# Adapter weights formed per sample and multiplied in two tiles of the array, in a four-layer conditioned network

## What is computed

```python
dg, db = c @ down_gamma, c @ down_beta        # [64, 64] each
ug, ub = c @ up_gamma,   c @ up_beta          # [64, 256] each
w_down = down_project[None] * dg[:, None, :] + db[:, None, :]     # [B, 256, 64]
w_up   = up_project[None]   * ug[:, None, :] + ub[:, None, :]     # [B, 64, 256]
up = einsum('bsh,bhd->bsd', relu(einsum('bsd,bdh->bsh', x, w_down)), w_up)
x = x + up
x = x + L1(x)     # x plus a product with weights of rank 30, decoded per sample
x = x + L2(x)     # a modulated projection, attention (16 heads, in each token), another projection
x = x + L3(x)     # table norms, three small networks, a gated two-layer network, a norm
```

## Time and profile before

| | |
|---|---|
| median of 3 runs | 538.26 us (537.77 to 538.40) |
| span of the profiled execution | 537.6 us |
| what the three runs have around that span | 0.2 to 0.8 us |
| PE busy | 462.3 us, 86% |
| DVE, ACT, POOL busy | 65%, 53%, 32% |
| moved by DMA | 61.0 MB, mean 113 GB/s |

### The profile page before, as it was taken

The page is one execution under the profiler, slowest core; times in us unless marked ns, Lnnn a source line. Parts: engine busy times, 40 slices in busy tenths (PEclk is TensorE's granted clock), DMA queues, the critical chain, the costliest instruction groups (busy, mean ns, idle before and its releaser), DMA issues.

```text
span 537.6 us, 9360 instructions
## 1 busy us (share of the span) xinstructions
PE 462.3 (86%) x3768; PEld 259.2 (48%) x3768; DVE 347.5 (65%) x653; ACT 282.6 (53%) x421; POOL 170.1 (32%) x146
## 2 busy tenths in 40 slices
PE   3896668924899999999999999999999898849981
PEld 3673335512365546554555654565546555424431
DVE  0374547593387488749856983898388778454923
ACT  0201488262853976578756966793976497102100
POOL 3009895110304232413231323314231420172121
PEclk9998767986599999999999999999999999879986
DMA  5991700331733713553183338143713561320011
GB/s 152 341 265 57 193 1 21 92 97 52 186 97 84 231 57 106 160 154 88 76 215 99 119 81 212 69 157 69 207 41 122 139 166 54 101 78 19 0 40 39
DMA packets 68736, 61.00 MB, mean 113 GB/s; under 512 B 53910, under 2 KB 55572, under 8 KB 68308
## 3 DMA queue, kind: packets, MB, share of 16 engines
q1 hardware_dynamic: 64404, 43.86, 30.0%
q0 software_dynamic: 3712, 12.59, 7.4%
q10 hardware_dynamic: 576, 3.95, 2.0%
HBM read 39.18 MB, written 21.07 MB: 112 GB/s over the span
## 4 chain that ended last, share of the span: by engine, by line
PE 67%; DVE 14%; issue 5%; DMA 5%; SPq 4%; ACT 3%; POOL 2%; POOLq 0%; DVEq 0%; ACTq 0%
PE ph L750 17%; PE pk L729 10%; PE pp L712 5%; PE ph L712 4%; PE ph L838 3%; PE pp L759 3%; PE pp L871 2%; PE pp L854 2%; DVE kx L1621 2%; PE pp L810 2%; PE pk L720 2%; PE pk L648 1%; PE ph L648 1%; PE pk L750 1%; DMA bd<-in_w_dec 1%
## 5 line engine op out<-in xcount | busy, mean ns | idle before, releaser
L1140 ACT ACTIVATE bd<-vc,ownrow 128x512 f32<-128x512 f32 x124 | 78.3, 711 | 0.0
L1127 ACT ACTIVATE bd<-kc,ownrow 128x512 f32<-128x512 f32 x120 | 75.6, 709 | 0.3
L447 POOL TENSOR_TENSOR demod<-demod,neghalf 128x32 f32<-128x32 f32 x8 | 43.4, 5448 | 35.2 <-DVE demod L1382 35.2
L729 PEld LDWEIGHTS pk<-bd,kc 128*32 128x32 f32 x1024 | 30.4, 120 | 17.1 <-issue 11.7
L729 PE MATMUL pk<-bd,kc 128*32 128x128 f32 x1024 | 35.4, 298 | 3.2 <-ACT bd L1127 3.2
L485 POOL TENSOR_TENSOR attnT<-attnT,style 128x1024 f32<-128x1024 f32 x6 | 11.4, 1901 | 76.4 <-DMA attnT<-av_dram 76.4
L712 PE MATMUL pp<-ys,kwT 128*128 128x512 f32 x64 | 30.6, 623 | 2.6 <-DVE ys L1604 2.6
L729 PE MATMUL pk<-bd,et 128*32 128x128 f32 x1024 | 31.1, 273 | 0.0
L729 PEld LDWEIGHTS pk<-bd,et 128*32 128x32 f32 x1024 | 27.2, 110 | 3.6 <-issue 3.2
L750 PE MATMUL ph<-tT,w 128*128 128x512 f32 x56 | 27.3, 633 | 0.1
L750 PE MATMUL ph<-x2T,w 128*128 128x512 f32 x56 | 25.9, 605 | 1.2 <-DVE h L1698 1.2
(11 more groups left out here) (348 smaller groups left out, 976.3 us busy)
## 6 DMA issues: line engine op xcount, KB each, us to landing
xin<-in_x SPq DMA_DIRECT2D x8, 512.0 KB, 4.5
x_dram<-x SPq DMA_DIRECT2D x8, 512.0 KB, 2.6
k_dram<-kxb SPq DMA_DIRECT2D x16, 256.0 KB, 3.3
kt<-k_dram SPq DMA_DIRECT2D x8, 512.0 KB, 4.0
v_dram<-kxb SPq DMA_DIRECT2D x8, 512.0 KB, 5.0
vt<-v_dram SPq DMA_DIRECT2D x8, 512.0 KB, 5.8
x1r<-x_dram SPq DMA_DIRECT2D x8, 512.0 KB, 3.5
av_dram<-av SPq DMA_DIRECT2D x8, 512.0 KB, 5.8
```

Of the source, the lines that this page charges most:

```text
L447: gp.tensor_tensor(q, q, neghalf[:, 0:4 * CB].rearrange("p (l a b) -> p l a b", l=2, a=2), ALU.pow).then_inc(gs_dem, 1)
L729: ins = mm(pk[32 * r:32 * r + 32, o:o + 128], weights(h, 4 * i + r)[:, 16 * pair:16 * pair + 32], bd[:, h, 8 * i + 2 * r + pair, :], start ...
L1127: fn(bd[:, h, :, 16 * b:16 * b + 16].rearrange("p (q z) x -> p q z x", z=2), kc[:, 16 * h:16 * h + 16, :].rearrange("p q (z x) -> p q z x" ...
L1140: fn(bd[:, h, :, 16 * b:16 * b + 16], vc[:, SH * h:SH * h + SH, :], ACT.Copy, scale=ownrow[:, 1, b:b + 1]).then_inc(s, 1)
```

## The change

- The factors of all samples are computed with samples on partitions, copied to `cond_rows`, stored to two DRAM tensors, and read back for each chunk broadcast over partitions: `down_gb` [128, 2, 512] by one transfer (512 KB) and `up_gb` [128, 2, 1024] by two transfers of 64 partitions (512 KB each). SP issues them at the end of step a for chunk a+1, the second pair after a wait on `p_up`.
- For each chunk GpSimd forms `w_down` (multiply, add; [128, 1024] each) and `w_up` (multiply, add; [128, 1024] each). Chunk 0's `w_down` is formed on DVE. Chunks 1 and 2 are formed between and behind the demodulation; chunk a+1 in steps a = 2 to 6: down behind the scaling of attnT, up behind the output store.
- The down product is 16 matmuls of 64 columns, alternating between two column tiles of 64; the up product 16 matmuls of 64 columns, alternating between two row tiles of 64. Relu is one ACT operation of 128x256 straight from PSUM. DVE adds 2x and the product in two operations (`stt`).
- The beta products, `row_in`, `row_mid` and their four DVE operations are gone, as are the columns of ones.
- `ys` shares `xT`'s buffer, `x1` shares `x0`'s, `kxb` shares `kx`'s; the waits move with them (`v_kx` now waits for both stores of the chunk before).
- In step 0 `first_factor(0)` and `(1)` come ahead of the down product.

```diff
+            sp.wait_ge(vs_par, 1)
+            sp.dma_start(down_dram.rearrange("g b h -> b g h"), cond_rows[:, 0:2 * H0].rearrange("b (g h) -> b g h", g=2)
+                         ).then_inc(d_rows, 16)
+            sp.dma_start(up_dram.rearrange("g b d -> b g d"), cond_rows[:, 2 * H0:].rearrange("b (g d) -> b g d", g=2)
+                         ).then_inc(d_rows, 16)
+            sp.wait_ge(d_rows, 32)
+            down_rows(0)
+            up_rows(0)
             for dst, src in late_loads:
...
                     sp.dma_start(xin[:, :, :], t["x"][:, (a + 1) * NT:(a + 2) * NT, :]).then_inc(d_x, 16)
+                    down_rows(a + 1)
+                    up_rows(a + 1)
...
+            def sample_down(c):
+                after(gp, d_dgb, c, 16)
+                after(gp, p_down, c - 1)
+                settled(gp)
+                gp.tensor_tensor(w_down[:, :, :].rearrange("p k (b h) -> p k b h", h=H0),
+                                 down_proj[:, :, :].unsqueeze(2).to_broadcast([128, 2, CB, H0]), by_sample(down_gb[:, 0, :]),
+                                 ALU.mult).then_inc(w_da, 1)
+                after(gp, w_da, c)
+                gp.tensor_tensor(w_down[:, :, :].rearrange("p k (b h) -> p k b h", h=H0),
+                                 w_down[:, :, :].rearrange("p k (b h) -> p k b h", h=H0), by_sample(down_gb[:, 1, :]),
+                                 ALU.add).then_inc(w_d, 1)
...
+            def sample_up(c):
+                after(gp, d_ugb, c, 32)
+                settled(gp)
+                gp.tensor_tensor(w_up.rearrange("p (b d) -> p b d", d=D), w_up.rearrange("p (b d) -> p b d", d=D),
+                                 up_proj[:, :].unsqueeze(1).to_broadcast([128, CB // 2, D]), ALU.mult).then_inc(w_ua, 1)
+                after(gp, w_ua, c)
+                gp.tensor_tensor(w_up, w_up, up_gb[:, 1, :], ALU.add).then_inc(w_u, 1)
...
+            gp.wait_ge(s_load, LAYERS)
+            sample_up(0)
             gp.wait_ge(vs_ss, 1)
-            demodulation(0, 4)
+            demodulation(0, 1)
+            sample_down(1)
+            sample_up(1)
+            demodulation(1, 4)
             networks()
             demodulation(4, NC)
             def step(n, a, v, d, e):
+                if a is not None and a == 1:
+                    sample_down(2)
+                    sample_up(2)
...
                                      ALU.mult).then_inc(g_ao, 1)
+                if a is not None and 1 < a < NC - 1:
+                    sample_down(a + 1)
...
                     gp.dma_start(out[:, e * NT:e * NT + NT, :], yn[:, :, :]).then_inc(d_out, 16)
+                if a is not None and 1 < a < NC - 1:
+                    sample_up(a + 1)
...
                     after(pe, a_xT, a)
+                    after(pe, w_d, a)
                     after(pe, v_hT, a - 3)
-                    for k in range(2):
-                        ins = mm(P0, w_down[:, k, :], xT[:, k, :], start=(k == 0), stop=(k == 1))
+                    for i in range(4):
+                        for k in range(2):
+                            for r in range(2):
+                                q = 4 * r + i
+                                ins = mm(P0[64 * r:64 * r + 64, S * i:S * i + S], w_down[:, k, H0 * q:H0 * q + H0],
+                                         xT[:, k, S * q:S * q + S], start=(i == 0 and k == 0), stop=(i == 3 and k == 1),
+                                         skip_group_check=True)
...
                     after(pe, a_act0, a)
+                    after(pe, w_u, a)
                     after(pe, a_hnT, a - 3)
-                    for o in range(2):
-                        mm(P23[:, 512 * o:512 * o + 512], w_up[:, 128 * o:128 * o + 128], act0, start=True, stop=True)
-                    mm(P0[64:128, :], w_up[:, D:D + H0], act0, start=True, stop=True).then_inc(p_up, 1)
+                    for i in range(4):
+                        for o in range(2):
+                            for r in range(2):
+                                z = slice(64 * r, 64 * r + 64)
+                                q = 512 * r + 256 * o + S * i
+                                ins = mm(P23[:, q:q + S], w_up[z, D * i + 128 * o:D * i + 128 * o + 128],
+                                         act0[z, S * i:S * i + S], start=(i == 0 and o == 0), stop=(i == 3 and o == 1),
+                                         skip_group_check=True)
...
-                if a is not None:
-                    after(pe, v_row_mid, a)
-                    for o in range(2):
-                        ins = mm(P01[:, 512 * o:512 * o + 512], ub_rows[64:128, 128 * o:128 * o + 128], row_mid, start=True, stop=True)
-                    ins.then_inc(p_ub, 1)
...
+                if a is not None:
+                    after(act, p_down, a)
+                    fn(act0[:, :], P0[:, 0:N // 2], ACT.Relu).then_inc(a_act0, 1)
                 if e is not None:
                     after(act, p_hid, e)
...
                     after(ve_, p_up, a)
-                    tt(by_batch(row_mid), by_batch(P0[64:128, :]), per_batch(batch_eye[64:128, :], B, a), ALU.mult
-                       ).then_inc(v_row_mid, 1)
-                    tt(by_batch2(x0[:, :, :]), by_batch2(halves(P23)), per_batch2(ug[:, :, :], a), ALU.mult
-                       ).then_inc(v_up, 1)
+                    after(ve_, d_x1w, a - 1, 16)
+                    for r in range(2):
+                        z = slice(256 * r, 256 * r + 256)
+                        stt(x0[:, :, z], xT[:, :, z], 2.0, P23[:, 512 * r:512 * r + 512].rearrange("p (o n) -> p o n", o=2),
+                            ALU.mult, ALU.add).then_inc(v_x0, 1)
```

More of the change, by code:

```diff
@@ L625, in _ @@
             pe.wait_ge(s_cond, COND)
[L627 to L630 removed]
+            mm(ph[0:B, 512:768], condT, ugam, start=True, stop=True)
+            mm(ph[0:B, 768:1024], condT, ubet, start=True, stop=True)
+            mm(ph[0:B, 0:64], condT, dgam, start=True, stop=True)
+            mm(ph[0:B, 64:128], condT, dbet, start=True, stop=True)
             for l in range(2):
@@ L642, in first_factor @@
                     pe.wait_ge(vs_par, 1)
+                    pe.wait_ge(vs_style, 4)
                 if i >= 2:
@@ L816, in step @@
                     hidden(0, hnT, p_hid, stop=True)
-                if a is not None:
-                    after(pe, v_row_in, a)
-                    settled(pe)
-                    mm(P1[0:H0, :], db_rows[64:128, :], row_in, start=True, stop=True).then_inc(p_db, 1)
-                    if first(a):
-                        first_factor(1)
                 if v is not None:
@@ L1202, in step @@
                     key_blocks(1, 4, 8, a_bk1)
-                if a is not None:
-                    after(act, v_t2, a)
-                    fn(act0, t1, ACT.Relu).then_inc(a_act0, 1)
                 if v is not None:
@@ L1373, in first_factor, with sample_down @@
                 ins.then_inc(vs_u, 1)
+            def sample_down():
+                ve_.wait_ge(d_dgb, 16)
+                tt(w_down[:, :, :].rearrange("p k (b h) -> p k b h", h=H0),
+                   down_proj[:, :, :].unsqueeze(2).to_broadcast([128, 2, CB, H0]), by_sample(down_gb[:, 0, :]), ALU.mult
+                   ).then_inc(w_da, 1)
+                ve_.wait_ge(w_da, 1)
+                tt(w_down[:, :, :].rearrange("p k (b h) -> p k b h", h=H0),
+                   w_down[:, :, :].rearrange("p k (b h) -> p k b h", h=H0), by_sample(down_gb[:, 1, :]), ALU.add
+                   ).then_inc(w_d, 1)
             def squares():
@@ L1559, in step @@
                         stt(yn[:, j, :], yn[:, j, :], rstd[:, 2, j:j + 1], x2k[:, j, :], ALU.mult, ALU.add).then_inc(v_yr, 1)
-                if a is not None:
-                    after(ve_, v_up, a)
-                    stt(x0[:, :, :], xT[:, :, :], 2.0, x0[:, :, :], ALU.mult, ALU.add).then_inc(v_x0a, 1)
-                    if first(a):
-                        first_factor(2)
                 if d is not None:
```

152 lines of the change are left out of this document (70 added, 82 removed).

## The result

The changed kernel takes **557.82 us** (median, 554.39 to 564.08) against 538.26. The ratio is **1.034, interval 1.029 to 1.038**: 3.4% slower, where 534.6 us was forecast, and outside the range. Now and then an execution of any kernel here, the one before included, takes up to 26 us longer; the ratios leave these out, the medians do not, and the traces shown of e6 and e11 are of such executions.

A forecast was written before the change was run, and what follows sets the result against it. The prediction took PE to set the pace in full steps; its terms summed to -3.65 us against the 537.6 us span, 533.95 profiled, and with the median 0.66 above that 534.6 us, range 527 to 547.

The forecast's parts named there:

- PE's sizes: Full steps on PE: down takes 1.2 us, up 1.9, and PE idles about 1.3 us ahead of `p_o`.
- Step 0: Down moves behind `first_factor(1)`, rows join the loads, the adapter's products give PE 4 us: -1.0 us, bounds -3 to +5.
- The clock had its own rival: Steps 3 to 6: the clock falls in PE's gaps, about 1.7 us lost per fall; 541.4 us in all, chance 0.18.
- Rows in step 0: Rival: the rows come late in step 0, +5 us for -1; 540.6 us in all, chance 0.06.
- Between steps 0 and 1: POOL forming chunk 1's weights holds L1396 in the networks' chain on DVE: +2.0 us, bounds 0 to +4.
- Step 1: Up-beta and its sum go, but the values wait for ACT's value blocks: -0.6 us.
- Step 2: A transfer chain decides before `p_o`; behind it up-beta goes and `x2T` starts before POOL's up work: -0.95 us.
- Steps 3 to 6: Full steps gain 0.4 us each, not 1.55, as POOL's up multiply delays `x2T`: -1.6 in all, bounds -6.2 to +8.
- the rival of 530.0: Steps 3 to 6: POOL does not meet `x2T`, so each gains 1.55 us; 530.0 us in all, chance 0.22.
- POOL's second operation between the two of `x2T`: Rival in steps 3 to 6: this adds 9.4 us over four steps; 544.0 us in all, chance 0.14.
- The forecast's own case: Steps 3 to 6: POOL's up multiply makes `x2T` wait from 250.7 to 252.1; 0.4 us gained per step, chance 0.36.
- Step 7: The last step, in which no weights are formed: -1.5 us.

The follow-up runs named there:

- e6: The changed kernel in its own order with 5 unread 512-column products ahead of first factor 0: 559.99 us, ratio 1.039.
- e11: The kernel before with unread 512-column products in four TensorE waits of steps 0 to 2, nothing of the change: 534.07 us, ratio 0.991.
- e3: The kernel before with only chunk 0's down product moved behind first factor 0 and 1: 565.87 us, ratio 1.051.
- e2: The kernel of e1 plus unread 512-column products, 5 ahead of first factor 0 and 8 ahead of the down product: 549.88 us, ratio 1.022.
- e1: The changed kernel with step 0 reordered on TensorE and DVE (first factor 0, 1, 2 ahead of the down product), no new work: 565.89 us, ratio 1.052.
- e4: The changed kernel with GpSimd waiting for `x2T` before it forms the up weights of chunks 3 to 7: 553.33 us, ratio 1.023.
- e9: The kernel of e7 with DVE's and GpSimd's start work reordered and three more loops of unread products on PE: 539.29 us, ratio 1.000.
- e10: The kernel of e9 with 6 unread products behind chunk 1's down product and 4 ahead of step 2's output projection: 540.41 us, ratio 1.003.
- e12: The kernel of e10 with chunk 1's down weights formed later on DVE, one unread product fewer ahead of the output product, none in step 2: 535.10 us.
- e7: The kernel of e2 with some early weight forming moved to DVE or later, e4's wait, and 4 and 4 unread products: 546.51 us, ratio 1.015.

## Why the prediction was wrong, step by step

- **PE's sizes: right.** Down 1.15 us (1.2 forecast), up 2.00 (1.9), the gap ahead of `p_o` 0.9 to 1.3 (1.3). The tiles overlap.
- **Step 0, -1.0 forecast, bounds -3 to +5, +15.0 measured: the step that failed.** "The adapter's five products give PE 4 us back" took every PE record of step 0 at the length it had before. The prediction named the moved down product and never asked what stood in its old place: in the kernel before, PE ran four records of 512 columns from 16.0 to 18.0, in the wait for the first weights, at the higher clock (1.96 us; 1.88 in step 4). After, it stood idle for 3.5 us there, and the step ran at 1.2 GHz. On PE before:

```profile
12.47 1.75 PE L759 MATMUL pp<-ident,xin 128*128 128x128 f32 x8
16.00 1.96 PE L810 MATMUL pp<-xT,w_down 128*128 128x512 f32 x4 [1.79 <-ACT xT L1172]
18.18 3.79 PE L648 MATMUL pk<-xnT,bd 128*128 128x64 f32 x32 [0.22 <-DMA bd<-in_w_dec]
```

  The eight transposes take 1.75 us, the last of them 0.27, its length at the higher clock, and the trace has the rise at 13.85. So there the clock rose ahead of the moved product, which then ran in the wait. In the changed kernel and in e3 none of the eight takes less than 0.42, up to 14.1 and 14.5 us, and the first rise on record is at 65.85 and at 74.96: no row shows the higher clock anywhere in step 0. That the order decides the whole time is shown, by all four executions of e3. How it acts on the clock is not: up to the transposes PE does the same in e3 and before, and the two traces differ already there. The clock had its own rival, but only in steps 3 to 6, at 1.7 us a fall. e3 shows the price of the order alone, e2 against e1 that of the clock, and e11's trace that of the clock in the order of before. Rows in step 0 were a rival too (+5, 0.06): they do come late, which e6 shows.
- **Between steps 0 and 1, +2.0 forecast, +3.4 measured.** The hold was right in kind and in size (1.7 us), at another instruction: the cast L1413 was held, not L1396's counterpart. The rest is the clock: from the rank-30 product to the scaling of `kx` it is 11.8 us for 9.9.
- **Step 1, -0.6: measured -0.6.**
- **Step 2, -0.95: measured +2.7.** The transfer chain decides, as said. From the issue of the attention output's store to that of the load behind it, it was 7.1 us where it was 5.3 before, and 5.3 and 5.8 in e2 and e4, so 1.8 of this may be of that execution; but step 2 takes 62.7 and 63.6 us in e2 and e4 too, 63.2 here and 60.5 before. The rest is `p_o` (5.99 us for 5.32) and `x2T` (2.21 us for 1.42, in e2 and e4 2.45 and 2.69), held by POOL's *down* work, which here runs late; the prediction had priced that work only against the soft-max product.
- **Steps 3 to 6, -0.4 each: measured +6.3, -1.4, -1.9, -1.7.** The meeting was worked out from rows landing 3.6 to 7.2 us behind their issue; in step 4 they took 8, and POOL came after `x2T`: the rival of 530.0. In step 3 two others came true together, the clock ahead of `p_o` (1.70 us, forecast 1.7) and POOL's second operation between the two of `x2T` (3.3 us with the wait for the first). They were priced apart, though the second comes only with the first (4 of 4 steps with a fall, 0 of 12 without, under e4). The forecast's own case, POOL's multiply delaying the first operation of `x2T` by 1.3 us at the full clock, occurred in none of the 16.
- **Step 7, -1.5: measured -2.1.**

Without the 15.0 us of step 0 and the 1.9 of clock behind it, the sum comes to 19.7 - 16.9 = +2.8, or 541 us: inside the range, but still slower where faster was forecast. That it comes so near is in part luck: in steps 3 to 6 a loss of 6.3 and gains of 5.0 leave +1.3 for the -1.6 forecast, and neither the loss nor the gains were those of the forecast.

## What to carry to other kernels

When work is moved or shortened, look at what stood in TensorE's waits before: a longer pause can cost it its clock, and all that follows pays (28 us here for two calls moved, 19 in e11's trace for a pause of 1.4 us). Read the clock from the length of a record that occurs elsewhere, above all before the first change in the clock column. And place a GpSimd operation of 2 to 3 us by semaphore behind the DVE operation that it could hold, since left to the landing of a transfer it meets it whenever something ahead makes the DVE operation late (4 of 16 steps here).

## What the runs showed of the hardware

- The Trainium skill, page "TensorE: Matmul & The Clock Gate", section "What's actually happening", states that the lower clock is the default and that activity releases it. The start agrees: the first transposes run at the lower clock (0.42 us each), and in the kernel before it is up at 13.85 us. But in e9 TensorE was busy for 19.7 us at 0.50, and in the changed kernel for 35 us with one pause of 1.9, both nearly all in records of 64 columns, and in e3 from 18.6 to 65.9 with pauses of 0.95 and 1.52 and products of 512 columns in it, and the clock did not rise in any of them; here the measurement decides. The same records kept the higher clock where it was up (e2, 19.4 to 29.7).
- A gap of 1.23 us was followed by the lower clock in step 3 of the changed kernel and not in e4. In e10 one of 1.55 was, in e12 one of 1.56 not; in e11 one of 1.37 was. What decides was not tried.
- GpSimd's streaming operations hold DVE operations with one tensor input too: the cast (2.15 for 0.42, 2.47 in e2) and `TENSOR_SCALAR` of 128x6 (1.93 for 0.23) and 128x384 (2.38 for 0.36). Over GpSimd's power operation the first two ran at their usual length in e7, and the third in the kernel before. The Trainium skill, page "SBUF — State Buffer", section "Who interferes with whom", lists cast and tensor-scalar among those that can take the shared ports. The trace agrees for streaming operations, not for the power operation.
- A broadcast of rows (512 KB), issued at 39.4 us behind the late loads, had landed at 55.7 in e10, 16.3 us later; the median of the eight such transfers of a run is 6.3 us there and 6.5 in the changed kernel.
